# A delta-rule scan with its operands exchanged, three wide products a step, evicted by VectorE

## The reference

```python
q, k, v = (short_conv(h @ W.T, w) for ...)       # h = layernorm(x); 4 taps, silu; 4 heads of 32
beta = sigmoid(h @ Wb.T)
# delta rule, chunks of 32 tokens, 8 chunks a batch
q, k = l2norm(q), l2norm(k);  v, kb = v * beta, k * beta
A = -(kb @ k.T) below the diagonal;  T = (I - A)^-1      # 32x32 for each head and chunk
u, w = T @ v, T @ kb
def step(S, (qi, ki, ui, wi)):                           # scan over the 8 chunks
    attn = lower(qi @ ki.T)
    u_i = ui - wi @ S
    o = qi @ S + attn @ u_i                              # -> delta
    S = S + ki.T @ u_i
short, longp = fir(v, 3 taps), fir(v, 63 taps)           # a filter for each of the 128 channels
paths = (short, longp, delta, v)
p = softmax(gelu([h, mean and var of the paths] @ W1) @ W2 / temp), floored
x = x + (rmsnorm(sum(p_i * path_i)) @ Wo.T)
x = x + sum of the two best of 8 experts: ((silu(h W11) * (h W12)) @ W2),  h = layernorm(x)
```

## Time and profile before

| | before |
|---|---|
| runs | 401.59 us median of 3 (397.64 to 405.42) |
| profiled execution | 399.36 us, span 397.5 us, mean granted clock 0.914 |
| PE busy | 338.5 us, 85% of the span, 6364 matmul records |
| DVE busy | 275.7 us, 69%, 679 instructions |
| ACT busy | 139.4 us, 35%, 257 instructions |
| POOL busy | 88.2 us, 22% |

### The profile page before, as it was taken

One profiled execution on the slowest core, in us unless ns is written; L12 is line 12 of the kernel. 1 busy time (PEld: TensorE's weight loads), 2 busy tenths in 40 slices (PEclk: granted clock), 3 DMA queues, 4 the chain that ended last, 5 costly groups with the idle time before them and its releaser, 6 DMA issues.

```text
span 397.5 us, 14307 instructions
## 1 busy us (share of the span) xinstructions
PE 338.5 (85%) x6364; PEld 254.6 (64%) x6364; DVE 275.7 (69%) x679; ACT 139.4 (35%) x257; POOL 88.2 (22%) x152
## 2 busy tenths in 40 slices
PE   6989986966884679888989779989889999889997
PEld 6344974645433566755766557768767668668886
DVE  2889963256828874977765599779736969859654
ACT  2243614130352224354512613544252454242221
POOL 6463000061445234400201423702100000300000
PEclk9899889885597578999999998999989999978999
DMA  7331443001111011110000103020000000000000
GB/s 242 157 107 28 110 75 115 5 3 31 17 13 28 4 30 17 16 27 2 3 2 2 31 3 44 0 41 5 2 28 4 4 0 2 1 0 5 23 2 26
DMA packets 42668, 12.47 MB, mean 31 GB/s; under 512 B 35440, under 2 KB 41712, under 8 KB 42480
## 3 DMA queue, kind: packets, MB, share of 16 engines
q1 hardware_dynamic: 39440, 9.47, 11.1%
q10 hardware_dynamic: 3168, 2.10, 1.7%
HBM read 8.68 MB, written 2.88 MB: 29 GB/s over the span
## 4 chain that ended last, share of the span: by engine, by line
PE 60%; DVE 21%; issue 7%; ACT 5%; POOL 3%; DMA 2%; SPq 0%; DVEq 0%; ACTq 0%
PE ps L592 18%; PE ps L486 13%; PE ps L635 11%; PE ps L531 9%; PE ps L516 4%; DVE v_room L1266 2%; DMA late_sb<-in_late 2%; DVE x L1285 2%; POOL g L430 1%; PE ps L667 1%; PE ps L659 1%; PE ps L686 1%; DVE pmean L1317 1%; DVE toep_room L1318 1%; DVE toep_room L1369 1%
## 5 line engine op out<-in xcount | busy, mean ns | idle before, releaser
L635 PE MATMUL ps<-w_sb,v_room 128*128 128x128 f32 x512 | 64.3, 280 | 4.3 <-DVE v_room L1266 2.2
L635 PEld LDWEIGHTS ps<-w_sb,v_room 128*128 128x128 f32 x512 | 62.1, 195 | 8.8 <-DVE v_room L1266 4.3
L592 PE MATMUL ps<-x_hi,w_sb 128*128 128x512 f32 x128 | 61.0, 477 | 5.3 <-issue 1.9
L1266 DVE TENSOR_TENSOR v_room<-toep_room,ps 128x512 f32<-128x512 f32 x64 | 43.3, 682 | 30.3 <-PE ps L592 16.0
L885 ACT ACTIVATE toep_room<-ps 128x512 f32<-128x512 f32 x64 | 38.0, 596 | 66.1 <-PE ps L592 56.9
L592 PE MATMUL ps<-x_lo,w_sb 128*128 128x512 f32 x128 | 52.5, 410 | 0.0
L592 PE MATMUL ps<-x_hi,w_lo 128*128 128x512 f32 x128 | 52.4, 410 | 0.0
L1285 DVE SCALAR_TENSOR_TENSOR x<-ps,rs,x 128x128 f32<-128x128 f32 x128 | 35.9, 342 | 10.2 <-PE ps L635 9.9
L396 POOL TENSOR_TENSOR rn<-ss,mh 128x16 f32<-128x16 f32 x8 | 23.1, 2902 | 64.9 <-DVE ss L1106 64.9
L430 POOL TENSOR_TENSOR g<-gm,mh 128x16 f32<-128x16 f32 x4 | 11.6, 2906 | 105.5 <-DVE gm L1386 105.5
L592 PEld LDWEIGHTS ps<-x_hi,w_sb 128*128 128x128 f32 x128 | 25.1, 196 | 14.7 <-DVE v_room L1266 3.8
(11 more groups left out here) (202 smaller groups left out, 582.1 us busy)
## 6 DMA issues: line engine op xcount, KB each, us to landing
toep_room<-in_toep SPq DMA_DIRECT2D x1, 1536.0 KB, 12.6
a_d<-a_hc SPq DMA_DIRECT2D x4, 256.0 KB, 3.0
v_room<-in_w SPq DMA_DIRECT2D x1, 1024.0 KB, 5.7
t<-t_d SPq DMA_DIRECT2D x4, 256.0 KB, 3.0
v_room<-in_w ACTq DMA_DIRECT2D x1, 1024.0 KB, 6.1
taps_room<-in_taps SPq DMA_DIRECT2D x1, 768.0 KB, 6.3
x_sb<-in_x SPq DMA_DIRECT2D x1, 768.0 KB, 9.4
out_y<-x ACTq DMA_DIRECT2D x3, 256.0 KB, 2.4
```

The lines of the kernel that those rows point to most:

```text
L592: ins = pe.matmul(bank[:, :], a[cols].bitcast(F32R), c[:, :].bitcast(F32R), start=(k == 0), stop=(k == 2))
L635: ins = pe.matmul(yb[:, P * j:P * j + P], fu[:, e % 2, f, P * j:P * j + P], w2_sb[:, FC * e + f, :], start=(f == 0), stop=(f == FC - 1))
L1266: dve.tensor_tensor(fu[:, e % 2, f, :], sg[:, i % 2, :], ps[VALUE[bank_of(p, i)]][:, :], ALU.mult).then_inc(s["fu_ready"], 1)
```

## The change

1. **The scan is transposed.** State and operands change sides: what was the right-hand side (32 columns) becomes the stationary one, and the constant matrices stand side by side as wide right-hand sides: `by_s = [wneg | q | identity]`, `by_u = [attn | kn]`. A step is 24 matmuls: 8 of 32 columns (`vb` by `t32_t`, emitted ahead of the wait for S), 8 of 96 columns (`s_sb` by `by_s`), 8 of 64 columns (`u_sb` by `by_u`). U, O and S of one step share a bank (2 and 4 in turn); S is carried on by the identity columns. DVE evicts: a transposition in 32x32 blocks to `u_sb`, one to `s_sb`, and one of the step's `o` to `delta_hc`. The ACT copies L1006, L1014 and L899 are gone.
2. **Blocks by transposes.** For pairs 0 and 1 (`DIRECT = 2`) DVE gathers the items with one strided transposition and one parity-weighted addition, and scatters them with two multiplications and one transposition. Pairs 2 and 3 still go through DRAM.
3. **Filters.** All 32 channels lie in two new lists for pair 0: channels 0 to 5 in `FIRST_START`, 6 to 31 in `FIRST_SCAN`, two in each entry as a rule.
4. **Order.** In the same lists stand `short_v` 1 to 3, `project_v` 2 and 3 of DVE, the two weight splits, the temperature (`temper`), the statistics and pair 1's scatter and `t16t`, which all stood elsewhere. In `SCAN`, `norm` is cut in three. ACT computes the temperature earlier; v has three buffers instead of two.

```diff
-FIR_FIRST = 24
+DIRECT = 2
...
-        [("gate", 1), ("sig", 1), ("value", 1), ("fuse", 1), ("norm", 0), ("gate", 2)],
-        [("sig", 2), ("value", 2), ("gate", 3), ("fuse", 2)], [("g", 0), ("weigh", 0)], [("g", 1), ("mask", 0)],
+        [("gate", 1), ("sig", 1), ("value", 1), ("norm_k", 0), ("fuse", 1), ("gate", 2)],
+        [("sig", 2), ("value", 2), ("gate", 3), ("norm_q", 0), ("fuse", 2)], [("g", 0), ("weigh", 0)], [("g", 1), ("mask", 0)],
...
+FIRST_SCAN = [[("fir", 6), ("fir", 7), ("beta_hc", 0), ("short", 3)], [("fir", 8), ("fir", 9), ("long", 0), ("norm_k", 0)],
+              [("fir", 10), ("fir", 11), ("norm_q", 0)], [("fir", 12), ("fir", 13), ("norm_kb", 0)],
+              [("g", 0), ("fir", 14)], [("g", 1), ("fir", 15), ("mask", 0)],
+              [("fir", 16), ("fir", 17), ("long", 1), ("reload", 0), ("split", 0)], [("fir", 18), ("fir", 19), ("temper", 0)],
+              [("fir", 20), ("fir", 21), ("centre", 0), ("square", 0)], [("fir", 22), ("fir", 23), ("long", 2)],
+              [("fir", 24), ("fir", 25), ("spread", 0), ("reload", 1)], [("fir", 26), ("fir", 27), ("centre", 3), ("square", 3)],
+              [("fir", 28), ("fir", 29), ("split", 1)], [("fir", 30), ("fir", 31), ("spread", 3), ("long", 3)],
+              [("next_scatter", 0), ("next_t16t", 0)], [("centre", 1), ("square", 1)]]
...
-                            ins = heads(ps[4], DH * k, DH, lambda q: t32_t[q, m, :], lambda q: vb[q, m, :],
-                                        start=True, stop=(n == 0))
-                            if n:
-                                ins = heads(ps[4], DH * k, DH, lambda q: wneg_t[q, m, :], lambda q: s_sb[q, k, :],
+                            ins = heads(scanned(n), COLS * k + U_COL, C, lambda q: vb[q, m, :], lambda q: t32_t[q, m, :],
+                                        start=(k == 0), stop=(n == 0))
+                        if n:
+                            pe.wait_ge(s_ready[n - 1], t1)
+                            for k in range(2):
+                                m = k * NC + n
+                                ins = heads(scanned(n), COLS * k, 3 * C, lambda q: s_sb[q, k, :], lambda q: by_s[q, m, :],
                                             start=False, stop=True)
...
+                            ins = heads(scanned(n), COLS * k + O_COL, 2 * C, lambda q: u_sb[q, k, :], lambda q: by_u[q, m, :],
+                                        start=False, stop=True)
...
+            def gather(u):
+
+                items_of[u](dve.transpose(t16_t[:, :, :], by_item(a_hc[:, :, :])))
+                high, low = (t16_t[:, :, HB * k:HB * k + HB].rearrange("p j i -> p i j") for k in range(2))
+                dve.scalar_tensor_tensor(a_it[:, :, :], low, parity[:, 1:2], high, ALU.mult, ALU.add).then_inc(s["a_made"], 1)
+
+            def scatter(u):
+
+                dve.wait_ge(s["t_items"], u + 1)
+                freed(dve, "y_done", u)
+                for k in range(2):
+                    ins = dve.tensor_scalar(y_sb[:, :, HB * k:HB * k + HB], t_it[:, :, :].rearrange("p i j -> p j i"),
+                                            parity[:, k:k + 1], None, ALU.mult)
+                items_of[u](ins)
+                dve.transpose(by_item(t16[:, :, :]), y_sb[:, :, :]).then_inc(s["t16_made"], 1)
...
+                        dve.wait_ge(s["u_done"], t * NC + n + 1)
+                        dve.transpose(u_sb[:, :, :], slots(n, U_COL)).then_inc(u_ready[n], 1)
+                    run(scan[2 * n])
+                    if t is not None:
+                        dve.wait_ge(s["s_done"], t * NC + n + 1)
+                        if n < NC - 1:
+                            dve.transpose(s_sb[:, :, :], slots(n, S_COL)).then_inc(s_ready[n], 1)
+                        delta_n = delta_hc[:, :, :].rearrange("p (k n) d -> p k n d", k=2)[:, :, n, :]
+                        ins = dve.transpose(delta_n, slots(n, O_COL))
```

More of the change, by code:

```diff
@@ L81 @@
         ("softmax", 0), ("fuse", 9), ("add", 3)]
[L83 to L89, removed]
 LAST_SCAN = [[item for item in items if item not in (("centre", 1), ("square", 1))] for items in SCAN]
@@ L334, in first @@
                                  t_it[64 * k:64 * k + 64, :, :]).then_inc(s["t_stored"], 16)
-                freed(sp, "y_done", u)
-                freed(sp, "t16t_ready", u)
-                sp.wait_ge(s["t_stored"], u * 32 + 32)
+                sp.wait_ge(s["y_done"], u)
+                sp.wait_ge(s["t16t_ready"], u)
+                sp.wait_ge(s["t_stored"], done * 32 + 32)
                 sp.dma_start(t16[:, :, :], t_d.rearrange("m p j -> p m j")).then_inc(s["t16_loaded"], 16)
-            first(0)
-            for u in range(1, NPAIR):
+            for u in range(DIRECT, NPAIR):
                 first(u)
@@ L999, in body @@
                 run(ahead)
[L1000 to L1016 removed]
+                for items in scan:
+                    run(items)
                 run(behind)
@@ L1135, in normalise, with by_item, turn16 @@
                 norm_kb(u)
+            items_of = [chained(dve, "item_vec", pair, ITEM_VEC) for pair in range(DIRECT)]
+            def by_item(a):
+                return a.rearrange("p m (k j) -> p j (m k)", k=2)
+            def gather(u):
[10 more added lines that the diff above has]
+                dve.transpose(by_item(t16[:, :, :]), y_sb[:, :, :]).then_inc(s["t16_made"], 1)
+                items_of[u].end()
+            def turn16(t):
+                t16_here(dve, t)
+                dve.transpose(flat(t16_t[:, :, :]), flat(t16[:, :, :])).then_inc(s["t16t_ready"], 1)
             def masks(u, chain):
@@ L1187, in _ @@
             project_v(1)
-            short_v(1)
             dve.wait_ge(s["pool_consts"], ALL_CONSTS)
@@ L1481, in parts_of @@
                                           ALU.subtract).then_inc(s["w_split"], 1)
-                steps = {"split": parts_of, "fuse": value, "add": down, "norm": norm, "mask": masked, "weigh": weigh, "centre": centre,
+                steps = {"v_hc": project_v, "short": short_v, "temper": temper, "next_scatter": lambda _: scatter(t + 1),
+                         "next_t16t": lambda _: turn16(t + 1), "split": parts_of, "fuse": value, "add": down, "norm": norm, "mask": masked, "weigh": weigh, "centre": centre,
                          "spread": spread, "stats": stats_out, "exp_in": exp_in, "softmax": softmax, "mix0": mix(0),
@@ L1500, in body @@
                 run(ahead)
-                for items in scan:
-                    run(items)
+                for n in range(NC):
+                    if t is not None:
+                        dve.wait_ge(s["u_done"], t * NC + n + 1)
+                        dve.transpose(u_sb[:, :, :], slots(n, U_COL)).then_inc(u_ready[n], 1)
+                    run(scan[2 * n])
+                    if t is not None:
+                        dve.wait_ge(s["s_done"], t * NC + n + 1)
[3 more added lines that the diff above has]
+                        ins = dve.transpose(delta_n, slots(n, O_COL))
+                        if n == NC - 1:
+                            ins.then_inc(s["delta_ready"], 1)
+                    run(scan[2 * n + 1])
                 run(behind)
             pipeline(body)
+            norm.end()
 _OUT = (B, L, D)
```

215 lines of the change are left out of this document (108 added, 107 removed).

## The result

The changed kernel takes 425.0 us (median of 4 runs, 422.9 to 426.6) against 402.0 us; the ratio is 1.061 with a 95% interval of 1.051 to 1.071. Forecast were 392.5 us and a range of 384 to 404.

The account below looks back on a forecast made before the run. PE was busy 85%, but in the first 105 us PE's and DVE's work stood one after the other. First pair -8.3 and later scans +1.5 made -6.8 us, from 399.36 to 392.5 us, range 384 to 404.

Parts of the forecast that it names:

- The later scans: Scans of pairs 1 to 3: +1.5 us together, as +1.5, -0.5 and +0.5, from evictions held behind DVE's long items.
- a quarter: Pair 1's scan: share of up to 10 us of late evictions taken to count, less 0.7 us for `t16t`: +1.5 us.
- The first rival: Later scans: DVE's queue is the bound, held evictions cost full length in pair 1, half after; +10, 401 us; chance 0.17.
- two signs of being wrong: Hops of pairs 1 to 3 waiting over 3 us a scan for DVE's queue; PE giving up its clock for longer.
- The argument that DVE is idle 31% of the time: Later scans: held against the skill's rule on a saturated DVE, which would make DVE's queue the bound.
- The first pair: Start through scan 0: PE's last product of scan 0 at 95.1 us instead of PE going on at 103.35, -8.3 us.
- The gather: Before scan 0: DVE gathers pair 0's blocks without DRAM, 48.3 us instead of 61.5; strided gather and scatter cost 2.7 us.
- PE is not late for it: Before scan 0: without 18 of 24 filter channels (11 us) PE is ready for u's first eviction at 58.2 us.
- Scan 0: First pair's scan: 38.9 us from 58.2 to 97.1, 9 us longer than the old; PE's last product at 95.1.
- The wait for the second weight load: Scan 0: `split(1)` needs a load of 6.1 us, so DVE holds back the hops for 3.6 us.
- The price of an eviction: All scans: a DVE transposition of 64 columns costs about 0.15 us; lower bound 0.1, rival 0.4 us.
- The slower rival: All scans: 92 evictions at 0.4 us each instead of 0.15 give +11 us, 410 us; slower from 0.25 us; chance 0.08.

Follow-up runs that it names:

- e1: The changed kernel with the old scan, evicted by ScalarE, in pairs 1 to 3: 397.7 us, ratio 0.988 to the kernel before.
- e2: The changed kernel with ScalarE evicting the new products by plain copies in pairs 1 to 3 (numbers not the reference's): 395.9 us, ratio 0.986.
- e4: The kernel before with u and S copied to SBUF by VectorE instead of ScalarE: 421.9 us, ratio 1.046.
- e9: The changed kernel with the comparisons, products and count of weigh left out: 405.4 us, ratio 1.013 to the kernel before.
- e10: e1 with the comparisons, products and count of weigh left out: 398.2 us, ratio 0.989 to the kernel before.
- e8: e3 with the blocks of all four pairs going through DRAM as before, filters still in scan 0: 410.5 us, ratio 1.022.
- e6: e1 with one lag of three run for filter channels 6 to 31 in scan 0: 390.6 us, ratio 0.975 to the kernel before.
- e3: The changed kernel with the old scan in all four pairs; gathers, filters and tables as changed: 396.7 us, ratio 0.987.
- e11: The kernel before with 24 more matmuls at its start, moving PE's code 96 places back: 408.5 us, ratio 1.015.
- e7: e1 with 24 more matmuls at its start, moving PE's code 96 places back: 404.9 us, ratio 1.009 to the kernel before.
- e12: The changed kernel with 24 more matmuls at its start: 425.7 us, ratio 1.058 to the kernel before.

## Why the prediction was wrong

**The later scans: +1.5 forecast, +24.9 measured.** This is the step that failed. I had the right mechanism, the three evictions behind `out` and `ln_cen`, the mask and `weigh`, and took "a quarter" of their 10 us with the argument that PE has expert matmuls ahead of most hops. That cover was not costed. PE's work ahead of the hop shown above is 2.3 us, against an item of 5.2; PE's direct waits for evictions grew by 17.1 us in the three scans, of which the sum had 1.5. (A quarter of 10 less 0.7 is 1.8, too.) The first rival had the same mechanism and a chance of 0.17. By its own condition, 10 us in pair 1 and half of it in pairs 2 and 3, it adds up to +20 and about 411 us; I had written +10 and 401, so that it stood as "no change". On top of the waits come the stretches at half clock behind the long ones, which I had not priced; two signs of being wrong that I had named came true here: the hops wait 7.7, 6.5 and 8.0 us a scan, where 3 was the limit, and PE's clock is lower for longer. e1, e2, e4, e9 and e10 show this cause from five sides.

**The argument that DVE is idle 31% of the time** was the wrong measure. The page's share says nothing on a hop: an eviction needs its engine at one moment, and ScalarE, at 35%, had no item above 1.3 us in the scans of pairs 1 to 3. The Trainium skill's advice ("Perfetto Trace Analysis", section "Optimizing Scalar/DVE Operations") to offload VectorE when it is saturated came out right in its direction, though at 70% VectorE was not saturated.

**The first pair: -8.3 forecast, +0.95 measured.** The gather was nearly right (48.3 against 50.5 us, and e8), though gather and scatter took 3.5 us instead of 2.7, the strided transpositions 1.03 and 1.04 each. "PE is not late for it" failed: the first u came at 64.25 instead of 58.2, later than the 62 us that I had named as a sign of being wrong, and 3.7 us of this are DVE's wait for PE with its stalls. The page showed such stalls ahead, 7% of the chain as "issue", and I gave them no price. Scan 0 was forecast at 36.9 us up to PE's last product and took 41.2: the 26 channels were priced by their 53 ns, without the stalls (3.09 and 2.29 us above) that stand in such short matmuls. I had costed the filters as work that DVE's items hide in most of the halves; e6 shows that PE sets the stage in the main. The wait for the second weight load, 3.6 us in the sum, was only 0.77.

**The price of an eviction** was too low, but not by much: 0.21 to 0.25 us from start to end, where I had 0.15, and the next instruction starts 0.17 us after it. The 0.38 for 128x256 on which the 0.15 rests is half of a row of two that overlap; a single one takes 0.42. For 23 evictions that is 1.4 to 2.3 us a scan at most. The products were right (e2: its three scans are 3.0 us shorter in sum than before, none of it in pair 1). The slower rival asked for 0.25 us or more of the engine for each eviction; e9 has the same evictions at the same price and gets most of the loss back, so the wait for DVE's turn is what counts.

**What stays open.** Whether the 1.2 to 1.3% by which e1 and e3 beat the kernel before belong to the gather and the tables, or to the place of PE's code: e11 moved the kernel before by 1.5% with nothing but such a shift and a delay of 1 us. By how much each of the three items holds the later scans: only `weigh` was taken out alone. What DVE's evictions cost in scan 0 (e3), and where e7 lost its 7 us.

## What to carry to other kernels

An eviction on a serial hop belongs to the engine that has nothing long queued around it, whatever its busy share: count for each hop the longest instruction group that can stand ahead of it, and set against it the work that the waiting engine has until then. A wait of PE is to be priced together with the matmuls at half clock that can follow it. Where a gap is closed, ask what had been hidden in it and where that goes.

## Not expected of the hardware

In the first pair PE has stalls without a releaser of 0.6 to 3.1 us in stretches of 20 to 53 ns matmuls. The one that was followed moves with the code, by 96 places in its stream for a shift of 96, in e7 and in e12; other stalls stand still. Such stalls made 4.4 of the 8.0 us by which the first eviction of u came later in e11. A wait of PE of 2.51 us was followed by 2.5 us at a granted clock of 0.50, and 16 records that take 2.05 us at full clock took 3.30.
